# One-core GNN and feed-forward kernel: order of loads and of work on a second weight copy at the beginning

## The reference, cut to what matters

```
ln(x)    = (x - mean) / sqrt(var + 1e-5)
gat(x,W) : h = x @ W.T, split in heads;  a_src = <h, att_src>,  a_dst = <h, att_dst>   per node and head
           e = leaky_relu(a_src[src] + a_dst[dst], 0.2);  alpha = softmax of e over the edges of one dst
           out[dst] = sum of alpha * h[src], + bias
x = x + gat(relu(gat(ln(x), W1: 1024x768, 8 heads of 128)), W2: 768x1024, 1 head of 768)
x = x + ffn(ln(x))     patch rows: gelu(x @ fc1.T + b) @ fc2.T + b;  the first 6 rows go through a gated pair of 5 "atoms"
```

## Time and profile before

| | us |
|---|---|
| median of 3 runs | 703.23 (703.04 to 705.6) |
| the profiled execution's own time | 700.96 |
| its span in the trace | 699.1 |
| PE busy | 686.3 (98% of the span) |
| DVE busy | 511.6 (73%) |
| ACT busy | 441.0 (63%) |
| POOL busy | 124.3 (18%) |

### The profile page before, as it was taken

One profiled execution on the slowest core, in us unless ns is written; L12 is line 12 of the kernel. 1 busy time (PEld: TensorE's weight loads), 2 busy tenths in 40 slices (PEclk: granted clock), 3 DMA queues, 4 the chain that ended last, 5 costly groups with the idle time before them and its releaser, 6 DMA issues.

```text
span 699.1 us, 13750 instructions
## 1 busy us (share of the span) xinstructions
PE 686.3 (98%) x4757; PEld 645.8 (92%) x4757; DVE 511.6 (73%) x866; ACT 441.0 (63%) x900; POOL 124.3 (18%) x150
## 2 busy tenths in 40 slices
PE   8899999999999999999999999999999999999997
PEld 6699999789999999999999899999998999999997
DVE  6887875999899999999998754434668643837232
ACT  6666766388999999999999744454361434422202
POOL 2151130001121202121121000000243330333302
PEclk9999999999999999999999999999999999999999
DMA  8737998979344334333323231101973544315102
GB/s 282 228 79 197 265 280 226 212 196 286 67 88 83 87 63 107 70 76 83 70 22 70 74 114 60 59 1 43 312 220 110 166 136 155 99 59 187 35 23 69
DMA packets 54430, 88.37 MB, mean 126 GB/s; under 512 B 17763, under 2 KB 37081, under 8 KB 54378
## 3 DMA queue, kind: packets, MB, share of 16 engines
q1 hardware_dynamic: 43798, 65.69, 33.4%
q0 software_dynamic: 6080, 8.17, 7.4%
q10 hardware_dynamic: 4500, 13.82, 5.9%
HBM read 68.09 MB, written 15.33 MB: 119 GB/s over the span
## 4 chain that ended last, share of the span: by engine, by line
PE 86%; DVE 4%; ACT 4%; DMA 3%; issue 1%; ACTq 1%; POOL 0%; SPq 0%; DVEq 0%
PE bank L1490 19%; PE bank L1630 13%; PE bank L1451 12%; PE bank L1554 12%; PE bank L1347 9%; PE bank L1734 4%; PE bank L1706 3%; DMA w1n_sb<-in_W 3%; PE bank L1264 2%; PE bank L1608 2%; PE bank L1760 1%; DVE x2f L2379 1%; PE bank L1497 1%; PE bank L1496 1%; ACT w_hi L1050 1%
## 5 line engine op out<-in xcount | busy, mean ns | idle before, releaser
L1490 PE MATMUL bank<-PT,h1s 125*128 125x250 f32 x660 | 147.5, 374 | 0.0
L1490 PEld LDWEIGHTS bank<-PT,h1s 125*128 125x128 f32 x660 | 121.2, 190 | 13.6
L2144 DVE SCALAR_TENSOR_TENSOR L<-asb,nad 125x1250 f32<-125x1250 f32 x80 | 120.8, 1545 | 0.8 <-PE bank L1451 0.7
L2155 DVE CUSTOM_DVE_ANT_0 L<-L,LC 125x1250 f32<-125x1250 f32 x80 | 114.2, 1459 | 1.3
L965 ACT ACTIVATE L<-L,nm 125x1250 f32<-125x1250 f32 x80 | 109.7, 1373 | 6.1 <-DVE nm L2155 4.8
L1451 PE MATMUL bank<-ident,L 125*125 125x125 f32 x800 | 94.0, 273 | 0.0
L1451 PEld LDWEIGHTS bank<-ident,L 125*125 125x125 f32 x800 | 91.1, 189 | 0.8 <-issue 0.4
L986 ACT COPY PT<-bank 125x500 f32<-125x500 f32 x165 | 83.8, 618 | 2.7 <-PE bank L1451 2.7
L778 POOL DMA_DIRECT2D PT_diff<-PT x34 | 28.4, 837 | 158.2 <-ACT PT L986 158.2
L1953 DVE TENSOR_TENSOR hot<-iota,edges 125x750 f16<-125x750 f16 x100 | 46.9, 542 | 9.1 <-PE bank L1264 5.9
L1630 PE MATMUL bank<-h_hi,PT_hi 125*125 125x384 f32 x200 | 41.5, 349 | 0.0
(11 more groups left out here) (289 smaller groups left out, 1341.1 us busy)
## 6 DMA issues: line engine op xcount, KB each, us to landing
asb<-src_logit_rows SPq DMA_DIRECT2D x14, 416.5 KB, 3.6
atom_w<-in_atom_inT SPq DMA_DIRECT2D x5, 1152.0 KB, 13.0
atom_w<-in_atom_outT SPq DMA_DIRECT2D x5, 1152.0 KB, 9.9
log_count_scratch<-LCw SPq DMA_DIRECT2D x10, 546.9 KB
LC<-log_count_scratch SPq DMA_DIRECT2D x10, 546.9 KB
LCt<-log_count_scratch SPq DMA_DIRECT2D x10, 546.9 KB
h_scratch<-h1st ACTq DMA_DIRECT2D x10, 448.0 KB
PT_diff<-PT POOLq DMA_DIRECT2D x34, 122.1 KB, 3.0
```

Source lines behind the costliest of these rows:

```text
L1490: mm = pe.matmul(sums, h1s[q][:, s, :], PT[p][:, s, :], start=(s == (0 if plain else PART + 2)), stop=(plain and s == NT - 1))
L2144: dve.scalar_tensor_tensor(L[s % RING][:, :], asb[q][0:NP, 1, :], nad1[:, ds(h, 1), t:t + 1].rearrange("p h t -> p (h t)"), asb[q][0:NP, 0 ...
L2155: dve.tensor_tensor_reduce(out=L[s % RING][:, :], in0=L[s % RING][:, :], in1=LC[:, t, :], scale=-1.0, scalar=-FLOOR, op0=ALU.add, op1=ALU.min,
```

## The change

ACT asks for W1 transposed directly behind its half of the edge lists, without waiting for `consts_made` and for all edge lists. Natural W1 comes in two transfers of four heads each. ACT's first activation (L809, which loads a table) comes behind these issues. The second copy of `iota2` (L818) moves behind `first_turned`, and `means(2)` behind `log_counts(0)`. SP asks for tile 2's rows when the first half of natural W1 is in, instead of the last third of W1 transposed. PE does part 0 of tile 1's first two pieces ahead of its wait for natural W1, all of part 1 of them behind it, and `turn(2)` and a piece of part 2 ahead of `first_columns`. DVE makes the first sixth of `w1_lo` ahead of the one-hots of tile 0 and the second one behind them, in front of the register loads of `plan_of(1)`. The amount of arithmetic and the bytes moved are the same.

```diff
--- before.py
+++ after.py
@@ -401,7 +401,8 @@
 
 
         consts_made = sem("consts_made")
-        att1_in, att_in, w1n_in, w2n_in, w2_in = (sem(n) for n in ("att1_in", "att_in", "w1n_in", "w2n_in", "w2_in"))
+        att1_in, att_in, w2n_in, w2_in = (sem(n) for n in ("att1_in", "att_in", "w2n_in", "w2_in"))
+        w1n_in = [sem(f"w1n_in{part}") for part in range(2)]
         w1_in = [sem(f"w1_in{i}") for i in range(KD // 2)]
         ffn_in, bias_in, edges_in = sem("ffn_in"), sem("bias_in"), sem("edges_in")
         attz_set = sem("attz_set")
@@ -498,7 +499,7 @@
             sp.dma_start(att2[:, 1, :], ad2T).then_inc(att_in, 16)
             sp.wait_ge(w1_in[0], 16)
             load_x(1)
-            sp.wait_ge(w1_in[2], 16)
+            sp.wait_ge(w1n_in[0], 16)
             sp.wait_ge(xn_ready, 1)
             load_x(2)
             sp.dma_start(b1_sb[:, :], b1c).then_inc(bias_in, 16)
@@ -805,17 +806,17 @@
         def _(act):
             for a, b in ROWS:
                 act.dma_start(srci[a:b, :], src_cols[a:b, :]).then_inc(edges_in, 16)
-            act.wait_ge(consts_made, 4)
-            act.activation(rstd[:, NT - 1:NT], tiny[:, :], ACT.Ln, bias=tiny[:, 0:1], scale=2.0)
-            act.wait_ge(edges_in, 3 * TWO)
             for k in range(0, KD, 2):
                 act.dma_start(w1_sb[:, k:k + 2, 0:HC], W1T.rearrange("(k p) n -> p k n", p=128)[:, k:k + 2, :]
                               ).then_inc(w1_in[k // 2], 16)
-            act.dma_start(w1n_sb[:, :, :], W1.rearrange("(h c) d -> c h d", c=C)).then_inc(w1n_in, 16)
+            for h in range(0, H, H // 2):
+                act.dma_start(w1n_sb[:, h:h + H // 2, :], W1.rearrange("(h c) d -> c h d", c=C)[:, h:h + H // 2, :]
+                              ).then_inc(w1n_in[h // (H // 2)], 16)
+            act.wait_ge(consts_made, 4)
+            act.activation(rstd[:, NT - 1:NT], tiny[:, :], ACT.Ln, bias=tiny[:, 0:1], scale=2.0)
             act.wait_ge(consts_made, 8 + 2 * SUB)
             act.copy(iota2[:, :, 0].rearrange("p (w r) -> p w r", w=SUB),
                      iota1[:, 0:NP].unsqueeze(1).to_broadcast([CE, SUB, NP])).then_inc(consts_made, 1)
-            act.copy(iota2[:, :, 1], iota1[:, :]).then_inc(consts_made, 1)
 
             def normalise(t):
                 p = t % 2
@@ -916,15 +917,16 @@
 
             centre_first()
             first_turned()
+            act.copy(iota2[:, :, 1], iota1[:, :]).then_inc(consts_made, 1)
             for k in range(KD):
                 act.wait_ge(w1_in[k // 2], 16)
                 act.copy(w1_hi[:, k, 0:HC], w1_sb[:, k, 0:HC]).then_inc(w1_hi_done, 1)
             means(1)
             centre(1)
-            means(2)
             features_out(0)
             rows_turned(1)
             log_counts(0)
+            means(2)
             centre(2)
             store_h1(0)
             load_x(4)
@@ -1390,7 +1392,9 @@
             pe.wait_ge(consts_made, 10 + 2 * SUB)
             pe.wait_ge(plan_ready, 1)
             count_edges(0, count_plan(0))
-            pe.wait_ge(w1n_in, 16)
+            products(1, parts=(0,), pieces=THIRDS[:2])
+            for part in range(2):
+                pe.wait_ge(w1n_in[part], 16)
             pe.wait_ge(attz_set, 3)
             pe.wait_ge(h1_out, 1)
             for h in range(H):
@@ -1398,17 +1402,16 @@
                     mm = pe.matmul(bank[5][32 * c:32 * c + 2 * H, 0:QW], attz[:, h, :], w1n_sb[:, h, c * QW:(c + 1) * QW],
                                    start=(h == 0), stop=(h == H - 1))
             mm.then_inc(wattp, 1)
-            products(1, parts=(0,), pieces=THIRDS[:2])
+            products(1, parts=(1,), pieces=THIRDS[:2])
             pe.wait_ge(watt_done, 1)
             for k in range(KD):
                 mm = pe.transpose(bank[5][:, 256 + 2 * H * k:256 + 2 * H * (k + 1)], wrow1[:, k * 128:(k + 1) * 128],
                                   ident[0:2 * H, 0:2 * H])
             mm.then_inc(wattp, 1)
-            products(1, parts=(1,), pieces=THIRDS[:1])
+            turn(2)
+            products(1, parts=(2,), pieces=THIRDS[:1])
             first_columns()
-            products(1, parts=(1,), pieces=THIRDS[1:2])
-            turn(2)
-            products(1, parts=(2,), pieces=THIRDS[:2])
+            products(1, parts=(2,), pieces=THIRDS[1:2])
             products(1, pieces=THIRDS[2:])
             count_edges(1, count_plan(1))
             inside = {2: ((2, 6), 2), 3: ((1, 7), 3), 4: ((0, 7), 4), 5: ((2, 6), 6), 6: ((1, 7), 7), 7: ((0, None), 8)}
@@ -1932,6 +1935,15 @@
             dve.scalar_tensor_tensor(edges_of(0, 1), dstf[:, :], float(SUB), qc[:, :], ALU.mult, ALU.add).then_inc(rows_set, 1)
 
 
+            def weights_lower(k):
+                dve.wait_ge(w1_hi_done, k + 1)
+                if k < KD - 1:
+                    dve.wait_ge(w1_used, k + 1)
+                else:
+                    dve.wait_ge(h1_full, 1)
+                dve.tensor_tensor(w1_lo[:, k, 0:HC], w1_sb[:, k, 0:HC], w1_hi[:, k, 0:HC].bitcast(F32),
+                                  ALU.subtract).then_inc(w1_lo_done, 1)
+
             def plan_of(t):
 
                 aways = dve.value_load(plan[0:1, t:t + 1], min_val=0, max_val=(1 << 2 * SUB) - 1)
@@ -1962,6 +1974,8 @@
                     dve.wait_ge(edge_step, 5)
                 if t + 1 < NT:
                     rows_of_edges(t + 1)
+                    if t == 0:
+                        weights_lower(1)
                     return plan_of(t + 1)
 
             def mend(t):
@@ -2039,9 +2053,11 @@
                 dve.tensor_copy(watt2[:, :, :], both).then_inc(watt_done, 1)
                 dve.tensor_copy(w2_sb[:, :, D:D + 2], both).then_inc(watt_done, 1)
 
+            weights_lower(0)
             dve.wait_ge(plan_ready, 1)
+            plan_0 = plan_of(0)
             dve.wait_ge(consts_made, 10 + 2 * SUB)
-            ahead = one_hots(0, *plan_of(0))
+            ahead = one_hots(0, *plan_0)
             dve.wait_ge(attz_set, 1)
             dve.wait_ge(att1_in, 16 * 2)
             spread = attz[:, :, :].rearrange("c h m -> c (h m)")
@@ -2049,14 +2065,8 @@
                 at0 = side * H
                 dve.tensor_copy(spread[:, at0:at0 + (2 * H + 1) * (H - 1) + 1:2 * H + 1], att1[:, side, :]
                                 ).then_inc(attz_set, 1)
-            for k in range(KD):
-                dve.wait_ge(w1_hi_done, k + 1)
-                if k < KD - 1:
-                    dve.wait_ge(w1_used, k + 1)
-                else:
-                    dve.wait_ge(h1_full, 1)
-                dve.tensor_tensor(w1_lo[:, k, 0:HC], w1_sb[:, k, 0:HC], w1_hi[:, k, 0:HC].bitcast(F32),
-                                  ALU.subtract).then_inc(w1_lo_done, 1)
+            for k in range(2, KD):
+                weights_lower(k)
             dve.wait_ge(wattp, 1)
             for c in range(4):
                 r = dve.tensor_copy(wrow1[:, c * QW:(c + 1) * QW], bank[5][32 * c:32 * c + 2 * H, 0:QW])
```

## The result

The changed kernel has a median of 704.80 us (703.66 to 708.1, 22 runs), the kernel before, run beside it, 703.82 us (700.99 to 706.06, 22 runs). The recorded ratio is 1.0026, interval 1.0014 to 1.0037: slower by a quarter of a per cent. The profiled execution took 705.25 us with a span of 703.3 us, against 700.96 and 699.1. In experiment 8 one run, and one of the kernel before beside it, took twice as long (1397.91 and 1397.65 us), and the medians leave them out.

What follows compares the result with a forecast made beforehand. PE, busy for 98% of the span, was taken to bound the kernel. 2.1 us won less 1.2 of delay = 0.9 gave 700.1 against the profiled 700.96, and 703.2 - 0.9 = 702.3 in the median; range 700.0 to 704.6.

Steps and rivals of the forecast that it cites:

- s = 1.2 us: Front: delay of tile 0's rows by W1's earlier request, passed on undiminished to first_products; taken as 1.2 us.
- the free value: Front: tile 0's rows not delayed by W1, s = 0, their transfer taking at most 3.5 us.
- the two waits that would show it: Front: DVE's idle time before L1831 and the start of first_products (11.95 + s), from which s is read.
- the bound of 3.4: Front: largest delay s allowed, 3.4 us, with tile 0's rows in at 3.22 + 6.9 = 10.1 us.
- that case, 703.3: Front: tile 0's rows wait behind W1, s = 2.1 to 2.6, gain about 0, 703.3 us; chance 0.22.
- The middle: PE's list up to count_edges(1): ends at about 42.0 instead of 44.07 us, 2.1 us won.
- natural W1 at 26.5: Ahead of the 64 small matmuls: natural W1 lands at 26.5 us, its requests going out 2.08 us earlier.
- the filling: PE's 2.60 us wait for natural W1 is filled with twelve matmuls of tile 1's part 0, counted 2.17 us.
- Tile 2's rows: Before turn(2): asked for later, they come at about 28 to 29 us, with slack of 1.6 us.
- DVE's order: Moved w1_lo steps: one_hots(0) starts at 17.3 as before, w1_lo complete at 28.6 to 30.7, costing nothing.
- The 0.60 us at 57: PE's idle time behind ACT at 57.04 us, from ACT's stores and logarithms; counted as 0, 0.6 at best.
- The offset: Whole kernel: the median lies 2.27 us above the profiled execution, carried over to the changed kernel.

Runs made afterwards that it cites:

- experiment 8: Changed kernel, but ACT waits for all edge lists, with table load and first activation ahead, before asking for W1; 699.19 us, ratio 0.9931 to the kernel before.
- Experiment 5: Changed kernel with 38 instead of 8 dummy turns of PE ahead of its wait in the front; 703.84 us, ratio 1.0008 to the kernel before.
- experiment 10: Kernel of experiment 8 with PE's order of work from the kernel before, so without the filling; 701.20 us, ratio 0.9973 to the kernel before.
- run 11: The kernel before, unchanged, executed once more for a second profile; this execution took 704.87 us.
- the repeat: The changed kernel, unchanged, run and profiled a second time; 705.39 us, ratio 1.0029 to the kernel before.
- kernel 9: Kernel of experiment 8, but ACT's request for W1 waits for POOL's small constants (3.2 us) instead of the edge lists; 699.59 us, ratio 0.9944 to the kernel before.
- experiments 6: The kernel before with 22 dummy turns of PE ahead of its wait for natural W1; 702.83 us, ratio 0.9989 to the kernel before.
- experiments 5 and 3: The 3: changed kernel, but ACT asks for tile 0's rows, in its own queue ahead of W1; 702.27 us, ratio 0.9984 to the kernel before.

## Why the prediction failed, step by step

**The step that failed** is "I take s = 1.2 us, nearer to the free value". The place, the mechanism and the two waits that would show it were named; the size was off. Between the statistics of before and of the five profiles with the request at 1.9 to 2.0 us (10.32 to 11.04) s is 3.6 to 4.3 us, above even the bound of 3.4. That bound priced tile 0's rows by the loaded request of the earlier trace rows (6.9 us), but in after these rows took 7.8 us: 3.0 until their first row moved, 4.1 until the last had, 0.7 until DVE read them. In before they had ended at 5.18, 1.6 us ahead of their use. Their price alone makes s. The last edge list was late too, by 1.1 to 1.5 us in four of the five and 0.7 in the fifth, but that added nothing: with the plan steps it would have let the statistics start at 5.46 + 2.80 = 8.26 in after, and DVE then stood 2.71 us for the rows. The reason given for 1.2 us, that the request meets W1's first megabyte at its start, spoke for the other side: just this first megabyte (0.70 to 0.98 MB of it) went ahead of all of tile 0's rows. The Trainium skill, DMA: Bandwidth & Descriptors, section Queues, rings and completion order, says that an engine drains a whole packet of one queue before it turns to the other. The packets of after agree with such turns once tile 0's rows have begun (40 rows of x beside 40 of W1 from 7 to 8 us); they don't from 4.97 to 6.27, where rows of x had been asked for and only W1 moved. The time that I gave that case, 703.3, was too low as well.

**A term that was missing.** That a front that is late leaves PE standing, and that the granted clock falls meanwhile, isn't in the sum: PE stood 3.0 to 3.35 us before L1242, and from the statistics to first_products it took 6.54 to 7.11 us in four profiles instead of 5.19, 1.35 to 1.92 more. Experiment 5 shows that the slow turns are the clock's. The Trainium skill, TensorE: Matmul & The Clock Gate, section What's actually happening, says that how many matmuls run at the low level differs between runs of one kernel; the traces agree (the twelve turns and turn(0) took 2.77 and 1.37 us in after, 2.42 and 1.46 in its second profile).

**The middle** was sized rightly: 0.37 us of idle time before part 0 (forecast 0.3), none before the 64 matmuls, and, counted from the end of count_edges(0), 17.08 us to the end of count_edges(1) instead of 18.91. That is 1.83 won where 2.1 were forecast; 42.0 was forecast for its end at s = 0, and experiment 8 has 41.97, with a front that is 0.27 early. But I named the wrong source for most of it. I had natural W1 at 26.5 by an earlier request, with a gain from the filling; experiment 10 has it by 26.1 with the request as late as before, and 1.54 of the 1.83 us without any filling. Its later request of tile 2's rows pays for part of that. By the packets the early request itself moved natural W1's end little in after (25.13, against 25.37 in experiment 8), though by 1.8 us in its second profile (23.62).

**Tile 2's rows** were in time (turn(2) at 39.12 in after, without a wait). **DVE's order** cost nothing: in experiment 8 the one-hots of tile 0 start at 17.25 (before 17.30), and w1_lo was never waited for. As foreseen, count_edges(1) waited for its last one-hots, 2.23 us instead of 1.98. **The 0.60 us at 57** went away in after (4.28 us late at 48, 3.76 at 60.80), counted as 0 in the forecast; by the end of the span 0.4 of it is lost again, and where wasn't looked for.

**The offset** of 2.27 us between the profiled execution and the median was carried over as a constant. It isn't one. The profile was of a run at the full clock; most runs of that kernel are not (701.4 us against 704.0 in the median), and run 11 shows what one of them loses: 1.54 us by transfers that are late, 1.60 by the clock. In profiles the change costs 4.2 us of span, in medians 1.0 (1.8 by the ratio, 2.1 in the repeat); kernel 8 wins 2.0 us of span and 4.8 us of the median (699.19 against 704.00 of the kernel before beside it). That the filling is what takes this loss away is not shown: kernel 10 keeps the clock without it. The two errors worked against each other: by the profiled times alone the forecast of 700.1 was 5.15 us too low, by the medians 2.5.

**Open**: why tile 0's rows began only when 0.70 to 0.98 MB of W1 were through; why kernel 10 is 1.6 us slower than kernel 9 in the median although their profiles have the same span of 697.7 us and their clocks are alike; what the slowest runs of experiments 6 and 10 are (707.18 us at a mean clock of 0.998, 705.33 at 1.000, 707.07 at 0.994); and where the last 0.4 us of the span went.

## What to carry to other kernels

Ask for a big transfer only when the small ones that the first chain of work needs have been asked for: here 1.3 us later was enough (its bytes then came when the small loads were nearly through), and 1.3 us too early cost five us of the first product's start. Look at the records of single packets, where a trace has them, before you call a first-come order shown. A wait of TensorE of 2 to 3 us can cost more than its length, since the clock may fall behind it. Look at the mean clocks of many runs before you carry over the distance from a profile to the median.

## What the runs showed of the hardware

- A transfer of 3 MB asked for 0.5 us ahead of tile 0's 0.38 MB on the other queue made these take 6.4 to 7.1 us from the end of their issue to their last packet instead of 2.0 (9.57 to 10.36 against 5.18, from 3.22); asked for at the end of their issue, it made them end at 5.60, and in before they ended at 5.12 to 5.58 in three profiles.
- Of that transfer 0.70 to 0.98 MB moved before the first row of tile 0 did; then the two queues took turns (40 rows of each from 7 to 8 us in after).
- A transfer asked for at 3.22 us moved its first packet at 4.91.
- ACT's queue issues transfers while the engine loads its table: the request at 1.97 us, the load from 1.90 to 3.18.
- The clock fell behind waits of TensorE of 3.02 to 3.35 us and not behind those of 1.04, 2.23 and 2.60 us before the 64 matmuls, but at the front it also fell behind waits of 2.00 and 2.14 us (experiments 5 and 3). The length of one wait doesn't decide it alone. In after it fell at 10.1 us, while TensorE stood from 9.6 on; in run 11 at 30.6, 1.3 us after TensorE had gone on.
